# Transposing x by copies inside SBUF and a 32x32 transpose on VectorE instead of on TensorE, in a fused attention block

## What is computed

```python
xn = layernorm(x, g_in)                       # x: (64, 128, 512)
q = (xn @ Wq).reshape(b, n, H, DH).transpose(0, 2, 1, 3) * scale
kv = xn @ Wkv                                  # 64 key and 64 value columns
sim = jnp.einsum('bhid,bjd->bhij', q, k) + bias
# causal mask, key mask, one null key in front
attn = jax.nn.softmax(sim, axis=-1)
out = jnp.einsum('bhij,bjd->bhid', attn, v)
out = out.transpose(0, 2, 1, 3).reshape(b, n, INNER) @ Wo
return x + layernorm(out, g_out)
```

## Time and profile before

| | |
|---|---|
| median of 3 runs | 1152.41 us (1152.06 to 1154.45) |
| the profiled execution's own time | 1154.45 us |
| its span, first to last instruction | 1154.5 us |
| busy: TensorE / VectorE / ScalarE / GpSimd | 1061.4 / 729.0 / 674.2 / 804.2 us |
| mean granted TensorE clock | 0.989 of 2.4 GHz |

### The profile page before, as it was taken

The page is one execution under the profiler, slowest core; times in us unless marked ns, Lnnn a source line. Parts: engine busy times, 40 slices in busy tenths (PEclk is TensorE's granted clock), DMA queues, the critical chain, the costliest instruction groups (busy, mean ns, idle before and its releaser), DMA issues.

```text
span 1154.5 us, 43028 instructions
## 1 busy us (share of the span) xinstructions
PE 1061.4 (92%) x14464; PEld 923.9 (80%) x14464; DVE 729.0 (63%) x3536; ACT 674.2 (58%) x2666; POOL 804.2 (70%) x1488
## 2 busy tenths in 40 slices
PE   4799999999999999999999999999999999999975
PEld 4678888888888888888888888888888888888864
DVE  4757666656666666766765766755766665666551
ACT  3656556566556556556655655656655656655651
POOL 2657777667777667777767777767777766777763
PEclk9999999999999999999999999999999999999987
DMA  8211211211221211220221121121121121121011
GB/s 224 64 40 49 67 57 40 66 61 45 68 65 31 67 60 47 66 67 31 65 66 44 65 66 41 55 66 56 50 68 51 45 67 58 48 66 47 30 39 36
DMA packets 51548, 67.72 MB, mean 59 GB/s; under 512 B 13888, under 2 KB 25664, under 8 KB 51392
## 3 DMA queue, kind: packets, MB, share of 16 engines
q1 hardware_dynamic: 49280, 63.21, 17.6%
q10 hardware_dynamic: 2112, 2.10, 0.6%
HBM read 40.11 MB, written 16.78 MB: 49 GB/s over the span
## 4 chain that ended last, share of the span: by engine, by line
PE 77%; ACT 8%; issue 6%; DVE 4%; POOL 1%; ACTq 0%; DVEq 0%; POOLq 0%
PE ps_pv L424 33%; PE ps_proj L430 32%; PE ps_s L387 7%; PE ps_pv L411 4%; ACT exp_bot L679 3%; ACT exp_top L679 2%; DVE o_lo L513 2%; ACT xt_hi L710 1%; DVE logit_bot L492 1%; PE ps_proj L448 1%; ACT o_hi L687 1%; ACTq L221 0%; DVEq L221 0%; DVE y_stats L521 0%; DVEq L225 0%
## 5 line engine op out<-in xcount | busy, mean ns | idle before, releaser
L679 ACT ACTIVATE exp_bot<-logit_bot,neg_max 128x129 f32<-128x129 f32 x512 | 201.7, 397 | 342.3 <-DVE neg_max L492 336.9
L430 PE MATMUL ps_proj<-xt_hi,wq_hi 128*128 128x256 f32 x1024 | 298.5, 292 | 4.1 <-DVE q_sb L568 3.9
L790 POOL TENSOR_TENSOR bias_b<-bias_c,mask_add 128x256 f32<-128x256 f32 (+1 forms) x512 | 289.6, 598 | 1.6 <-DVE neg_max L492 0.3
L492 DVE CUSTOM_DVE_ANT_0 logit_bot<-ps_s,bias_b 128x128 f32<-128x128 f32 x512 | 128.7, 289 | 255.4 <-PE ps_s L387 226.8
L430 PE MATMUL ps_proj<-xt_lo,wq_hi 128*128 128x256 f32 x1024 | 288.0, 281 | 0.0
L430 PE MATMUL ps_proj<-xt_hi,wq_lo 128*128 128x256 f32 x1024 | 287.9, 281 | 0.0
L424 PE MATMUL ps_pv<-wo_hi,o_hi 128*128 128x512 f32 x512 | 211.8, 414 | 51.1 <-DVE o_lo L513 51.1
L799 POOL TENSOR_TENSOR w_nrm<-exp_bot,w_inv 128x256 f32<-128x256 f32 x256 | 156.6, 612 | 120.0 <-DVE w_inv L501 118.8
L424 PE MATMUL ps_pv<-wo_lo,o_hi 128*128 128x512 f32 x512 | 204.9, 400 | 0.0
L424 PE MATMUL ps_pv<-wo_hi,o_lo 128*128 128x512 f32 x512 | 204.8, 400 | 0.0
L430 PEld LDWEIGHTS ps_proj<-xt_hi,wq_hi 128*128 128x128 f32 x1024 | 192.8, 188 | 14.3 <-issue 5.1
(11 more groups left out here) (61 smaller groups left out, 1850.7 us busy)
## 6 DMA issues: line engine op xcount, KB each, us to landing
x_in<-in_x_dram SPq DMA_DIRECT2D x32, 512.0 KB, 4.1
x_res<-in_x_dram SPq DMA_DIRECT2D x64, 256.0 KB, 2.8
out_dram<-y_out SPq DMA_DIRECT2D x64, 256.0 KB, 2.0
v_rep<-v_raw SPq DMA_DIRECT2D x256, 32.0 KB, 1.9
w_raw<-in_L_cond_Wq_dram ACTq DMA_DIRECT2D x4, 512.0 KB, 7.9
w_raw<-in_L_cond_Wo_dram SPq DMA_DIRECT2D x4, 512.0 KB, 6.1
mask_u<-in_mask_BxS_bk_dram SPq DMA_DIRECT2D x32, 32.0 KB, 3.7
bias_c<-in_fside_16xSxS_dram SPq DMA_DIRECT2D x4, 128.0 KB, 8.1
```

The costliest lines, as they stand in the source:

```text
L430: mm = pe.matmul(ps[:, 0:TOK], w[:, k, cols], xt[:, k], start=(j == 0), stop=(j == len(todo) - 1))
L492: ins = nc.vector.tensor_tensor_reduce(out_[:, e, 0:keys_], ps_s[e][:, from_:from_ + keys_], bias[:, e], -1.0, 0.0, ALU.add, ALU.min, neg_ ...
L679: ins = nc.scalar.activation(out_[:, s, j], in_[:, s, j], ACT.Exp, bias=neg_max[:, s, k:k + 1], scale=-1.0, accum_out=w_sum[:, s, k:k + 1])
L790: ins = nc.gpsimd.tensor_tensor(out_, bias, key_mask, ALU.add)
```

## The change

From the third group on, x is not transposed on TensorE. ScalarE writes `xn` with its 32-column blocks in another order (`x_norm`), SyncE spreads it by 16 copies of 32 KB inside SBUF into `x_split` (`split_x`), each from a 32-partition block to another, and one VectorE instruction transposes all 32x32 blocks into `x_turned` (128x1024, `turned`, step 6). ScalarE casts that to `xt_hi` (two instructions of 128x512, step 7), VectorE subtracts to `xt_lo` (two of 128x512, step 7). The first two groups still go over TensorE.

`x_in`, `xt_hi` and `xt_lo` get a second buffer. The statistics of x move to step 0 (mean and variance included), `x_rstd_of` stays at step 1 of the half by number (`STEP_STATS` + 1, with `STEP_STATS` now 0) and goes ahead of that step's `normalize`, and `x_norm` moves from step 7 to step 1. g_in is multiplied into Wq and Wkv while these are split, in pieces of 128 rows, so that xt needs no factor; in the start of the program the statistics and `x_rstd_of` of the second group move ahead of other work, the latter ahead of `causal_bias` on GpSimd. SyncE issues `split_x` of half 0's group first in a pair, and that of half 1's group after the second store. The load of half 1's x moves ahead of that store; the load for half 0 stays last in the pair.

```diff
-    1: [("q", 7, 0), ("x", 0, 1), ("x", 1, 1)],
+    1: [("q", 7, 0)],
...
-STEP_STATS, STEP_XN, STEP_V, STEP_MASK = 4, 7, 7, 7
+STEP_STATS, STEP_XN, STEP_XR, STEP_XT, STEP_V, STEP_MASK = 0, 1, 6, 7, 7, 7
...
+            def split_x(f):
+                wait(sp, xn_made, GB * (f + 1))
+                apart(sp)
+                wait(sp, x_turned_made, f - BY_PE)
+                apart(sp)
+                for a in range(N // BLK):
+                    for r in range(P // BLK):
+                        sp.dma_start(x_split[BLK * r:BLK * (r + 1), :, a],
+                                     xn[BLK * a:BLK * (a + 1), :, P * r:P * (r + 1)]).then_inc(ld_split, 16)
...
+                if not last:
+                    split_x(2 * p + 2)
                 if not first:
                     store(p, -2, True)
                 spread_v(2 * p + 1)
+                if not last:
+                    load_x_and_mask(p + 1, 1)
                 if not first:
                     store(p, -1, True)
                 if not last:
-                    load_x_and_mask(p + 1, 1)
+                    split_x(2 * p + 3)
                 store(p, 0, True)
...
+            def turned(f):
+
+                wait(dve, ld_split, 16 * SPLITS * (f - BY_PE + 1))
+                wait(dve, xt_lo_made, XT * f)
+                nc.vector.transpose(x_turned[:].rearrange("p k (a j) -> p a k j", j=BLK),
+                                    x_split[:].rearrange("p b a (k i) -> p (b a) k i", i=BLK)).then_inc(x_turned_made, 1)
+
+            def x_low(f, slot, i, from_pe):
+                x_raw, hi, lo = halves_of(f, slot, i, from_pe)
+                wait(dve, xt_hi_made, XT * f + i + 1)
+                nc.vector.tensor_tensor(lo, x_raw, hi.bitcast(F32), ALU.subtract).then_inc(xt_lo_made, 1)
...
                         if not last:
                             if t % CG == STEP_STATS:
-                                x_stats_of(2 * p + t // CG + 2)
-                            if t % CG == STEP_STATS + 1:
+                                x_stats_of(p + 1, t // CG)
                                 x_mean_var_of(2 * p + t // CG + 2)
+                            if t % CG == STEP_XR:
+                                turned(2 * p + t // CG + 2)
+                            if t % CG == STEP_XT:
+                                for i in range(XT):
+                                    x_low(2 * p + t // CG + 2, t // CG, i, False)
...
-                    if not last and t % CG == STEP_XN:
-                        x_norm(2 * p + t // CG + 2)
+                    if not last and t < CP:
+                        if t % CG == STEP_XN:
+                            x_norm(2 * p + t // CG + 2, t // CG)
+                        if t % CG == STEP_XT:
+                            for i in range(XT):
+                                x_high(2 * p + t // CG + 2, t // CG, i, False)
...
+            x_rstd_of(1)
+            pool.wait_ge(x_shift_made, 2)
             pool.wait_ge(bias_shifted, 2)
             causal_bias()
             masked_bias(0, 0, 0)
             masked_bias(1, 0, 1)
-            x_rstd_of(1)
...
+                    if not last and t < CP and t % CG == STEP_STATS + 1:
+                        x_rstd_of(2 * p + t // CG + 2)
                     if t < CP:
                         normalize(n, t)
-                    if not last and t % CG == STEP_STATS + 1:
-                        x_rstd_of(2 * p + t // CG + 2)
```

156 lines of the change are left out of this document (93 added, 63 removed).

## The result

The changed kernel is slower: 1214.3 us (median of 4 runs, 1211.58 to 1219.16) against 1153.28 us of the kernel before (4 runs, 1152.06 to 1154.45), a ratio of 1.0525 with a 95% interval of 1.0492 to 1.0558. The forecast was 1189 in a range of 1176 to 1214, so the measured time lies at its upper end: 1.0525 times the 1152.4 on which the forecast was built is 1213. The profiled execution took 1211.58 us with a span of 1209.6; before it was 1154.45 and 1154.5. So 55.1 us of span have to be found.

The account below looks back on a forecast made before the run. TensorE bounds the kernel, except before step 3's projection, where a chain over other engines does. 14.0 (half 1) + 19.6 (half 0) + 4.6 (start) - 2.1 (end): +36, 1189 us on the 1152.4 median; range 1176 to 1214.

Parts of the forecast that it names:

- the lock: Rival: in step 7 both xt_lo on VectorE wait until GpSimd's y_out ends; 16 us more, 1205 us; chance 0.16.
- The clock: Rival: TensorE's idleness before step 2's scores in half 0 halves its clock; 2.8 us each, 1228 us; chance 0.12.
- SyncE's queue: Copies inside SBUF at 0.59 us stay hidden; rival at 1.0 us each costs 110 us; chance 0.08, shared with late load.
- Half 1: x long loaded: statistics delay q7's copy, x_rstd and xn delay exp_bot and step 3's projection; +0.93 us, 15 times.
- Steps 6 and 7: New transpose, casts and xt_lo on VectorE and ScalarE exceed their 0.7 us cover by nothing; each us beyond costs one.
- Half 0: x, loaded last in the pair, lands after VectorE wants it, delaying step 3's projection; +1.4 us, 14 times.
- Start: GpSimd waits for the second group's x_rstd ahead of causal_bias, delaying the first logits; +4.6 us, bounds 3 to 6.
- End: The last pair's first half has neither transposes nor preparation of x; -2.1 us.

Follow-up runs that it names:

- e5_stats_early: Changed kernel with the statistics of x and x_rstd one half earlier, and x loaded earlier for it: 1123.2 us, 0.9728 of the kernel before.
- e1_low_pool: Changed kernel with xt_lo subtracted on GpSimd after its work of step 7 instead of on VectorE: 1194.3 us.
- e2_low_one_input: Changed kernel with xt_lo made on VectorE from one SBUF input instead of two, leaving x's low part out of the result: 1212.7 us.
- e3_stats_after_q7: Changed kernel with the statistics of x on VectorE behind the copy of q7 instead of ahead of it: 1245.6 us.
- e10_low_pool_pad8: e1_low_pool with eight one-column memsets ahead of everything on VectorE, shifting its loop by eight instructions: 1195.9 us.

## Why the prediction was right or wrong

**Direction and main cause: right.** Slower, because the statistics stand ahead of the copy of q7, and x_rstd and xn ahead of exp_bot of step 2. e5_stats_early takes the statistics and the wait for x_rstd out of the way, and a loss of 5.3% turns into a gain of 2.7%.

**The size: too small, and the range held by spare room that was there for something else.** Forecast were 3% and measured 5.3%. The upper end of 1214 was set for the lock (1212) and for parts of clock and queue; what filled it was a cost that no term and no rival names. That the range held is luck.

**Half 1: right.** +0.93 forecast, +1.14 measured; scores at 7.45 and 7.63, projection at 12.95 and 13.11. The rest is VectorE's start: logits at 1.60 instead of 1.26, since steps 6 and 7 took 0.35 more than their cover of 0.7. In e1_low_pool, without this, the projection of half 1 is at 12.95 on average (12.92 to 12.98). One length was too short without consequence: scores, PV and kv take 4.08 at the full clock (299.46 less 1.40 less 293.98), not 3.9, so the wait for o_lo is 1.40 and not 1.6.

**Steps 6 and 7: the step that failed.** "Cover 0.7 us, so I cost this at nothing" was wrong by the lengths and by what the sum left out. xt_lo was put at 0.6 and took 1.34 on average; the transpose, 1.21, and the cast, 0.62, were inside their bounds. This made VectorE late by 0.35 in half 1. In half 0 the sum left out the branch at the end of VectorE's loop: 3.15 to 3.38 us pass between it and VectorE's next instruction, 13 times, and 1.50 to 1.74 of them are seen as idle time. Here the length of xt_lo does not matter, since the branch stands behind the wait for xt_hi: in e2_low_one_input VectorE ends its loop 0.5 us earlier and the logits are at 3.20, against 3.24. The sum's rule, "each us beyond 0.7 costs one", is therefore right for half 1 and not for half 0. The trace of before gives no price for this, since there the next instruction follows the branch after 0.24 to 0.28 us in all 13 rounds; that this loop would fall on the other side could hardly be foreseen.

**Half 0: the term of +1.4 was too small by half, and its reason hardly acted.** Measured +2.82. x of half 0 landed as assumed, 4.0 us after its issue in the median (assumed 4.1) and at 6.3 of the half (assumed 6.3), but VectorE reached x_stats later than at 5.40, in the half shown at 7.2, and waited in only two of the loop's half 0 (0.65 and 0.22 us). Of the +2.82, 1.14 is what half 1 has too, and 1.7 is the late start after the branch. So far as +1.4 came near anything, that is luck. The reason is real all the same: it appeared in e1_low_pool, 1.04 us in the row shown, as soon as VectorE was on time. The difference of 1.42 in 14 halves is 20 us, and the forecast for the profiled execution was 21 short (1190.5 against 1211.6).

**Start: too high**, 4.6 against 2.1. causal_bias started at 27.04, as forecast (27.0), but took 3.75 us in place of 5.10, and the first logits that need the bias were 3.3 later; at the end of the first half 1.8 of this was left.

**End: right**, -2.1 against -1.86, with 1.0 more in the last half.

**The lock: both engines were longer beside each other, but the price was not as told.** A pair of xt_lo went from 1.29 to 2.64 and y_out of step 6 from 1.29 to 1.61. Whether one stands still meanwhile or both are slowed, these times do not tell. But the forecast's sequence (both xt_lo only behind y_out) did not occur: the first got in between. Its 1205 us counted 0.75 in half 1; measured was 0.2. For half 0 the length of xt_lo did not matter (e2_low_one_input).

**The clock: it fell in more than half of the halves, but cost little,** because the slow stretch lies beside the chain over xn. That the clock can halve is in the traces: windows of 0.50 stand beside windows of 1.00, before too (0.50 at 1118 to 1120). The rival counted 2.8 us per half 0, with the clock low for all of the 3.9 us of work; in the half shown it was at 0.50 from 549.1 to 552.0 and at 1.00 from there on. Where it is exposed, in e3_stats_after_q7, it costs 1.5 us in a half 1 and up to 2.5 in a half 0.

**SyncE's queue** was hidden in the changed kernel, as forecast, at 0.65 to 0.72 us per copy (forecast 0.59).

## What to carry to other kernels

Before counting a removed operation as a gain, ask what was waiting behind it: here 0.95 us of transposes were worth 0.33, since a copy of VectorE ended just as late. An operation that is moved joins two queues, that of its engine and that of the engines that use its result; check whom it now stands in front of at each. And look at what stands ahead of an engine's loop branch. Here a shift of the loop by eight instructions made its code be fetched again in every round (18 packets in e1_low_pool, 83 in e10_low_pool_pad8), which took 2.71 to 3.01 us there and 3.15 to 3.38 in the changed kernel. In e10_low_pool_pad8, where the branch started 3.0 to 3.6 us before the next scores, the time did not move by it (1195.9 against 1194.3); it left 1.50 to 1.74 us of idle time a round in the changed kernel, where the wait for xt_hi stands ahead of the branch and it started 0.5 to 0.7 before them.
